# 66 more matmuls of ones at thirteen places of the first three tiles

## The reference, cut to what matters

```python
x = x + xattn0(layernorm(x), ctx, ctx)        # A: 32 query heads of width 8, 8 key/value heads, softmax
x = x + moe(layernorm(x))                     # B: 8 experts, top 2 by sigmoid score, and one shared expert
x = x + xattn1(layernorm(x), ctx)             # C: 16 heads of width 16, keys and values from ctx, causal
x = x + bitlinear_ffn(layernorm(x))           # D: weights to -1, 0, 1, activations to 8 bits, hidden 1024
```

## Time and profile before

| | us |
|---|---|
| median of 3 runs (lowest, highest) | 597.67 (597.24, 598.57) |
| profiled execution | 598.97 |
| its span, first to last instruction | 597.24 |
| TensorE busy | 515.1 (86%) |
| VectorE, ScalarE, GpSimd busy | 373.4, 361.7, 280.7 |
| mean granted TensorE clock | 0.946 |
| TensorE's part of the chain of waits | 59% |

### The profile page before, as it was taken

How to read it: one execution, slowest core, us unless ns; L and a number is a source line. 1 busy time by engine, 2 the same in 40 slices (tenths; PEclk the granted TensorE clock), 3 DMA queues, 4 the chain that set the end, 5 groups by cost and what they waited for, 6 DMA issues and landing times.

```text
span 597.2 us, 10760 instructions
## 1 busy us (share of the span) xinstructions
PE 515.1 (86%) x3825; PEld 325.6 (55%) x3838; DVE 373.4 (63%) x816; ACT 361.7 (61%) x707; POOL 280.7 (47%) x535
## 2 busy tenths in 40 slices
PE   5275889899998998999999899999998999997765
PEld 2141445557465656565746565664656565775442
DVE  3463654665776567487667677577587358736554
ACT  5034453546583758569684947685667566855653
POOL 3967642445365336363625535462542542544230
PEclk9666879999997999999999999999999999999697
DMA  5878521312232112224131320432030212006000
GB/s 170 182 199 211 142 77 32 89 44 61 76 100 66 43 31 72 79 66 110 30 87 39 102 43 18 113 75 60 25 97 10 66 43 68 9 12 159 10 11 19
DMA packets 66445, 43.98 MB, mean 74 GB/s; under 512 B 36616, under 2 KB 61064, under 8 KB 66392
## 3 DMA queue, kind: packets, MB, share of 16 engines
q1 hardware_dynamic: 60064, 37.56, 24.6%
q10 hardware_dynamic: 6328, 5.73, 3.5%
HBM read 30.49 MB, written 12.39 MB: 72 GB/s over the span
## 4 chain that ended last, share of the span: by engine, by line
PE 59%; ACT 18%; DVE 11%; DMA 6%; issue 2%; POOL 2%; SPq 1%; POOLq 0%; ACTq 0%
PE big L649 20%; PE small L682 9%; ACT PA L877 5%; PE small L628 5%; PE small L747 2%; PE small L795 2%; PE small L586 2%; DMA ctxT<-in_ctxT 2%; DVE neg_maxA L1201 2%; PE big L601 2%; PE big L718 2%; PE small L765 2%; PE big L723 2%; DMA parts_qA<-QP 1%; ACT PC L877 1%
## 5 line engine op out<-in xcount | busy, mean ns | idle before, releaser
L1201 DVE TENSOR_REDUCE neg_maxA<-big 128x8 f32<-128x1024 f32 x64 | 76.5, 1215 | 21.8 <-PE big L601 21.4
L901 ACT ACTIVATE tB<-big,route_half 128x128 f32<-128x128 f32 x128 | 36.5, 370 | 73.2 <-PE big L649 73.2
L1105 POOL TENSOR_TENSOR vB<-vB,route_c 128x512 f32<-128x512 f32 x32 | 33.6, 1051 | 86.1 <-DVE vB L1260 85.8
L877 ACT ACTIVATE PA<-big 128x1024 f32<-128x1024 f32 x64 | 63.7, 1035 | 12.3 <-PE big L616 11.7
L682 PE MATMUL small<-w2T,hTB 128*128 128x256 f32 x288 | 65.6, 382 | 1.0 <-ACT hTB L914 0.7
L649 PE MATMUL big<-w1T,xTB 128*128 128x512 f32 x128 | 64.1, 625 | 2.3 <-DVE vB L1253 2.3
L649 PE MATMUL big<-w3T,xTB 128*128 128x512 f32 x128 | 60.1, 592 | 0.0
L682 PEld LDWEIGHTS small<-w2T,hTB 128*128 128x128 f32 x288 | 53.7, 190 | 9.4 <-issue 1.8
L1113 POOL TENSOR_SCALAR_AFFINE_SELECT PC<-PC 128x1024 f32<-128x1024 f32 x32 | 35.0, 1100 | 27.8 <-ACT PC L877 27.8
L1201 DVE TENSOR_REDUCE neg_maxC<-big 128x8 f32<-128x1024 f32 x32 | 38.4, 1212 | 15.0 <-PE big L723 15.0
L1221 DVE SCALAR_TENSOR_TENSOR tB<-tB,big 128x512 f32<-128x512 f32 (+1 forms) x48 | 26.3, 547 | 26.9 <-ACT tB L901 26.7
(11 more groups left out here) (194 smaller groups left out, 1183.3 us busy)
## 6 DMA issues: line engine op xcount, KB each, us to landing
parts_qA<-QP SPq DMA_DIRECT2D x16, 192.0 KB, 2.4
QA<-parts_qA SPq DMA_DIRECT2D x32, 96.0 KB
parts_kC<-KPC SPq DMA_DIRECT2D x16, 192.0 KB, 2.1
KC<-parts_kC SPq DMA_DIRECT2D x16, 192.0 KB, 2.9
parts_qC<-QPC SPq DMA_DIRECT2D x16, 192.0 KB, 2.1
QC<-parts_qC SPq DMA_DIRECT2D x16, 192.0 KB, 2.9
x<-in_x SPq DMA_DIRECT2D x16, 128.0 KB, 2.5
QA<-parts_qA SPq DMA_DIRECT2D x32, 64.0 KB
```

What stands on the lines that cost most here:

```text
L877: return op(dst[:, 8 * j:8 * (j + 1), :], ps[:].rearrange("p (h t) -> p h t", t=P), ACT.Exp, scale=scale).then_inc(S[name], 1)
L901: ins = op(tB[:, (e0 + i) * HID:(e0 + i + 1) * HID], ps[:, i * HID:(i + 1) * HID], ACT.Tanh, scale=rt["half"][:, e0 + i:e0 + i + 1])
L1105: g.tensor_tensor(hB[:, sl].rearrange("p (e h) -> p e h", e=4), vB[:, sl].rearrange("p (e h) -> p e h", e=4), rt["c"][:, e0:e0 + 4].unsque ...
L1201: v.tensor_reduce(dst[:, 8 * j:8 * (j + 1)], ps[:].rearrange("p (h t) -> p h t", t=P), FREE, ALU.max, negate=True).then_inc(S[name], 1)
```

## The change

Thirteen entries are added to the table of matmuls of ones, for parts of tiles 0, 1 and 2: 22 before A2.0/0, 3 each before A2.2/0 and A2.3/0, 6 before A2.0/1, 3 each before A2.2/1 and A2.3/1, 4 before S2.0/0, 3 before A4.0/0, 4 before A5.0/0, 6 before A4.0/1, and 3 each before A6.0/0, A2.0/2 and A2.2/2: 66 in all. Nothing else changes, neither an order nor a wait nor a result.

```diff
 FILL = """
-    A1/1:4 S1.0/0:3 C9/15:3 D2/14:1 D1/15:2 D3/14:5 D4/14:4
+    A1/1:4 S1.0/0:3 A2.0/0:22 A2.2/0:3 A2.3/0:3 A2.0/1:6 A2.2/1:3 A2.3/1:3 S2.0/0:4 A4.0/0:3 A5.0/0:4 A4.0/1:6
+    A6.0/0:3 A2.0/2:3 A2.2/2:3 C9/15:3 D2/14:1 D1/15:2 D3/14:5 D4/14:4
     """
```

## The result

The kernel with the 66 matmuls takes 594.63 us (median of 22 runs, 593.29 to 597.98), beside 597.68 for the kernel before (22 runs). The ratio is 0.9946 with a 95% interval of 0.993 to 0.9963: faster by 3.05 us between the medians, 0.5%. (A ratio here is not the quotient of the two medians, which is 0.9949.) Ratios leave out executions that are more than 1.5% above the fastest of their kernel. The forecast was 596.3 with a range from 594.8 to 599.4; the sign was right, the size was not.

What follows compares the result with a forecast made beforehand. TensorE, busy 86% of the span, bounds it, with dense work at half clock. Terms +0.7 - 1.3 + 0.2 - 1.6 = -2.0 us; for the median -1.2 from 597.67 gives 596.5, said as 596.3; range 594.8 to 599.4.

Steps and rivals of the forecast that it cites:

- the price of one: Each further matmul of ones on TensorE costs 0.215 us at the high clock, 0.425 at the low.
- The early group: Entries up to A4.0/0: the 22 are worth 0, and A4.0/0 begins at 44.8, +0.7 us (bounds +0.2 and +2.5).
- A5.0/0 to A6.1/0: Tile 0 up to A6: high clock makes A6.1/0 end at 58.5 against 59.09, -0.6 us with the +0.7 included.
- a term put at nothing: Before A5.0/0 and A4.0/1: four and six matmuls cost nothing more; the maxima rows' landing moves from 54.6 to 55.3.
- at worst: Before A4.0/1: the six take 2.55 us, ending at 55.3, just at the landing of the maxima rows.
- A5.0/1 and A5.1/1: A5 of tile 1: at the high clock takes 1.85 us instead of 3.44, -1.6 us.
- the halving: A5 of tile 1: only half of the -1.6 us is taken for the median, since other executions may lack that low stretch.
- Rival (1): Pause before A5.0/0 still drops the clock, only A5 of tile 1 gains: no change that can be told, 597.5; chance 0.33.
- Rival (2): Matmuls ahead of released work (A2.0/1, A4.0/0, A6.0/0) are not hidden: slower, +2.0 us, 599.6; chance 0.22.

Runs made afterwards that it cites:

- after: The kernel before with all 66 matmuls of ones added (the full change): 594.63 us, ratio 0.9946.
- before again: The kernel before itself, unchanged, run again as a control and for a second trace: 598.86 us, ratio 1.001.
- the six: The kernel before with only 3 matmuls before A2.0/2 and 3 before A2.2/2 added: 597.67 us, ratio 1.0001.
- after again: The kernel with all 66 run again, beside its parts on one chip: 595.3 us, ratio 0.9944.
- the 22 alone: The kernel before with only the 22 matmuls before A2.0/0 added: 598.23 us, ratio 1.0004.
- the early group: The kernel before with only the eight entries up to A4.0/0 added (47 matmuls): 597.3 us, ratio 0.9985.
- w2T later: The kernel before with the load of w2T and sw2T issued after both copies of A5 of tile 0: 598.41 us, ratio 1.0006.
- the late five: The kernel before with only the five entries from A5.0/0 on added (19 matmuls): 596.35 us, ratio 0.9978.
- the 56: The full change without the ten matmuls before S2.0/0, A4.0/0 and A6.0/0: 594.63 us, ratio 0.9948.

## Why the prediction was right or wrong

**What bounds it, and the price of one: right.** The 22 took 4.91 us, 4.7 and a latency; the six before A2.0/1, at the low clock, 2.48. That matmuls of ones count for the clock is shown by the same 66 at 8 columns, which leave it at 0.950 in the mean where the full ones bring 0.971. The sentence that what is won is not taken back by another engine holds for the most part: of 4.0 us won at A5.1/1 in the pair of profiles, 3.6 reach the end. One reading was wrong: of the three dense stretches at the low clock I put two on the chain, while the chain, which has TensorE from 37.2 to 44.5, from 54.6 and from 65.0, has all three. The terms were summed as if it had, and nothing hangs on it.

**The early group: right.** A2.0/0's 22 end at 21.1, as said, and are worth nothing that can be told, alone or beside the others. (A2.0/0 followed them at once, so QA had landed by then, and not at 22.3: that landing too is the execution's own.) VectorE's sixth maximum ended at 41.04 (41.0 said), C2.1/0 began at 38.78 (38.6) and took 1.1, A4.0/0 began at 45.10 (44.8): +1.0 for the +0.7. In another execution it was +2.8, for which I had given a bound of +2.5.

**A5.0/0 to A6.1/0: a term put at nothing.** I said 58.5, it was 56.45: -2.6 and not -0.6. The length is as summed, 3.3 us from A4.0/1 to A6.1/0 for my 3.2. What failed is the step before it: that the landing of the maxima rows moves from 54.6 to 55.3 with the rest, so that A5.0/0 and the six in front of it gain nothing at any clock. (The reason given, that it shares a queue with the load of w2T, was wrong as well: that load is issued by ScalarE, the rows by SP. They share the DMA engines, at a share of 0.99 over 48.2 to 50.7.) In fact the clock held over the pause, A5.0/0 took 1.06 us for 1.93 and the six 1.47 for the 2.55 of "at worst"; they were done at 53.1, no wait for the rows followed, and both are on the chain of waits of after (start, length, what held it):

```profile
50.71 1.06 PE small L629 x8
51.78 1.40 PE big L413 x6
```

But part of the 2.6 is chance. The second trace of the kernel before shows that 54.6 was the execution's own; there A6.1/0 ended at 57.48. Over the traces that are one kernel up to there, A6.1/0 ends at 58.3 in the mean without the change (before, before again, the six) and at 57.1 with it (after, after again, and the two with five before B5.1/0). So the term was -1.2, twice my -0.6, and the other 1.4 of the pair of profiles are chance.

**A5.0/1 and A5.1/1: the mechanism right, the halving wrong.** They took 1.92 for 3.51. I carried -0.8 of -1.6 to the median, since I took the low clock there for a mishap of the profiled execution. Of six traces of kernels without the late ones, it was low there for the most part in five (2.90 to 3.64: before twice, the 22 alone, the early group, w2T later) and high in one (1.92: the 66 at 8 columns); 3.1 in the mean, so -1.2 was to be carried and not -0.8. It was high in every trace that has the three before A2.2/2. With that term alone the sum would have said -1.6; with the other as well, -2.2, which is 595.5.

**Rest.** Put together, A5.1/1 ends at 67.8 in the mean of two traces of before and at 65.5 in four with the change: -2.3, where my sum had -1.2. From there to B6/0 it is 22.4 and 22.2 us before, 22.95 and 22.97 after, so 0.6 is taken back where my sum had nothing, and -1.7 is left. The other 1.4 of the 3.05 us I can't place. Single long executions don't explain them: three of the 22 of the kernel before are over 602 us (on four other chips 11 of 119 are at a mean clock of 0.932 to 0.935 and 601.5 to 603.9 us, while none of the 34 of after is under 0.960 or over 598.1), but without those three its median is 597.64 and not 597.68. What may be a part of them, and isn't shown, is that the two traced executions of after are no typical ones: both are above the median of their kernel's runs (595.31 against 594.63, 598.08 against 595.3), and both belong to the traces with B6/0 at 87.8 or later, which need 0.7 us or more longer from there on than those of the other kind.

**The rivals.** Rival (1), the clock falls in the pause before A5.0/0 all the same, did not hold in after: it was at 1.00 over 48.2 to 50.7. It did hold in the late five (fall at 49.3) and the 56 (49.6), which have the same four. So the rival was near, and I can't say by what it lost: the seven before S2.0/0 and A4.0/0 go with a clock that holds, but the busy time ahead of the pause is the same without them. (Its own price didn't follow from its sum: +0.6 against the profiled execution, put at 597.5, 0.2 below the median.) Rival (2), matmuls ahead of released work, is real by its price: with the 56, A4.0/0 began 0.8 earlier. It was outweighed. The order rule of the Trainium skill (TensorE: Matmul & The Clock Gate, The mechanism) agrees with the timelines shown here, and did not decide. Its other sentence (What's actually happening), that the number of slow matmuls varies from run to run, agrees too: the clock's first rise after the pauses was at 34.5 in one trace of after and at 40 in the other. I drew the wrong thing from it, that a gain seen in one profile should be cut for the median; the median gained more than any term of mine.

**The range** missed by 0.2 us at its lower end. That end already held the whole of the -1.6 and 0.9 more, so the halving isn't what it lacked: it had no room for the term that was put at nothing, nor for the 1.4 that no trace places. That it missed by so little is no sign that its terms were right.

## What to carry to other kernels

Work without use can pay where TensorE idles shortly before dense work, and it has to be tried as one thing with the work around it: the late five alone and the early eight alone gave nothing that can be told, together 0.5%. A fixed stretch of time compares two profiles badly once the work in it has moved; count from the event that matters. Such work costs nothing only where the operands come later still, and it wins nothing where the next work isn't on the chain (the 22). And of a wait on a transfer, one trace gives one draw: a second trace of the same kernel moved it by 2.1 us, which was more than the term that rested on it. Nor is a traced execution the median one: look where it stands among the runs.

## What was not expected of the hardware

- After the same busy time (2.4 of 3.2 us) and the same pause (1.8 us) the granted clock held in seven traces and fell in two. It fell as early as 0.4 us after TensorE's last matmul (the early group) and as late as 2.4 (the 22 alone).
- Between 92 and 545 us the clock falls once in every trace but w2T later, which has three such falls: at 182 to 192 us for some 7 us in before, before again and the six, and elsewhere, for about half as long, in the others. In before it follows a wait of 1.72 us that ends at 184.4, and then lasts through 7 us of dense work.
- The last maxima rows before A4.0/1 took 6.76 us to land in the kernel before; between two executions of it A4.0/1 began 2.1 us apart, at the end of that wait in both, while A4.0/0 began 0.2 us apart.
- The best version run is the full change with five more before B5.1/0: 592.59 and 593.25 us, ratios 0.9904 (0.9866 to 0.9942) and 0.9925 (0.9901 to 0.995). It beats the kernel before in both. It was never run beside after on one chip; the ratios 0.9925 and 0.9904 stand against 0.9946 and 0.9944.
